# A four-layer cross-attention kernel: the third layer (layer 2) loads the context's means and variances that layer 0 stores

## What is computed

```python
# layer 0
q_c = _ln(x) @ W_qc + b_qc
kv_c = _ln(context) @ W_kvc + b_kvc          # _ln: (x - mean) * rsqrt(var + 1e-6), no weights
# layer 2
xq = _ada_ln(x_q, t_vec, Wss_q, bss_q)
xkv = _ada_ln(x_kv, t_vec, Wss_kv, bss_kv)   # (x - mean) / sqrt(var + 1e-5), then (1 + scale) * . + bias
kv = (xkv @ Wkv + bkv).reshape(B, Lkv, 2, nh, dh)
# layer 3 attends to the context as it is, with no norm of it
```

## Time and profile before

| | |
|---|---|
| median of 3 runs | 5429.4 us (5426.66 to 5432.44) |
| the profiled execution | 5426.89 us, its span 5425.1 us |
| modulation and phase `pa` (layer 0) | up to about 1819 us of the span |
| expert layer (layer 1) | 1823 to 2403 us |
| phase `pb` (layers 2 and 3) | 2407 us to the end |
| busy share of the span | PE 86%, DVE 76%, ACT 66%, POOL 31% |
| DMA | 17% of the 16 engines' span, 50 GB/s |

### The profile page before, as it was taken

How to read it: one execution, slowest core, us unless ns; L and a number is a source line. 1 busy time by engine, 2 the same in 40 slices (tenths; PEclk the granted TensorE clock), 3 DMA queues, 4 the chain that set the end, 5 groups by cost and what they waited for, 6 DMA issues and landing times.

```text
span 5425.1 us, 123295 instructions
## 1 busy us (share of the span) xinstructions
PE 4676.3 (86%) x47956; PEld 2196.8 (40%) x47956; DVE 4123.3 (76%) x8997; ACT 3587.5 (66%) x4899; POOL 1673.2 (31%) x2339
## 2 busy tenths in 40 slices
PE   4689889889998588867989999999999998989987
PEld 2234433433433377752333333333333343333333
DVE  4588888888878244445888888888888887887884
ACT  1377777777777344423777777777777777777776
POOL 3444343343341100024232423233222223232321
PEclk9799999999999899986999999999999999999998
DMA  2211211211210111102112111121211111211110
GB/s 52 68 52 54 68 44 54 67 44 52 61 39 25 45 33 33 33 25 64 52 51 66 55 58 55 53 66 54 67 56 53 51 48 50 62 43 53 42 46 7
DMA packets 362976, 271.12 MB, mean 50 GB/s; under 512 B 47911, under 2 KB 325002, under 8 KB 362396
## 3 DMA queue, kind: packets, MB, share of 16 engines
q1 hardware_dynamic: 362396, 263.23, 17.0%
HBM read 86.96 MB, written 12.78 MB: 18 GB/s over the span
## 4 chain that ended last, share of the span: by engine, by line
PE 36%; ACT 7%; DVE 6%; issue 5%; POOL 1%; SPq 0%; DMA 0%; ACTq 0%; POOLq 0%; DVEq 0%
PE pb_obank L1021 13%; PE pb_dbank L1034 8%; ACT pb_probs L772 6%; DVE pb_c_maxs L693 5%; PE pb_aunit L997 5%; PE pb_aunit L1068 2%; PE pb_aunit L1075 2%; PE pb_dbank L1082 1%; PE pb_aunit L1060 1%; PE pb_aunit L1108 1%; PE pb_aunit L1102 1%; PE pb_aunit L1005 1%; ACT pb_c_kf L815 1%; PE pb_aunit L1051 0%; PE pb_aunit L1092 0%
## 5 line engine op out<-in xcount | busy, mean ns | idle before, releaser
L693 DVE TENSOR_REDUCE pb_c_maxs<-pb_dbank 128x1 f32<-128x512 f32 (+1 forms) x3584 | 2044.5, 627 | 411.6 <-PE pb_dbank L1034 397.1
L772 ACT ACTIVATE pb_probs<-pb_aunit 128x1024 f32<-128x1024 f32 (+1 forms) x1792 | 1744.5, 1024 | 380.4 <-PE pb_aunit L997 344.8
L693 DVE TENSOR_REDUCE pa_c_maxs<-pa_dbank 128x1 f32<-128x512 f32 (+1 forms) x1792 | 1025.8, 627 | 180.2 <-PE pa_dbank L1034 170.5
L772 ACT ACTIVATE pa_probs<-pa_aunit 128x1024 f32<-128x1024 f32 (+1 forms) x960 | 934.8, 1026 | 198.1 <-PE pa_aunit L997 174.8
L1021 PE MATMUL pb_obank<-pb_probs,pb_c_vaug 128*9 128x256 f32 x13312 | 953.2, 384 | 6.3 <-ACT pb_probs L772 5.5
L1034 PE MATMUL pb_dbank<-pb_c_kst,pb_c_qst 62*128 62x512 bf16 (+1 forms) x4096 | 780.5, 344 | 77.1 <-DVE pb_c_maxs L693 67.7
L997 PE MATMUL pb_aunit<-pb_c_qst,pb_c_kst 64*128 64x256 bf16 x6144 | 570.1, 273 | 61.1 <-ACT pb_probs L772 43.1
L1034 PEld LDWEIGHTS pb_dbank<-pb_c_kst,pb_c_qst 62*128 62x128 bf16 x4096 | 233.6, 93 | 632.8 <-DVE pb_c_maxs L693 433.2
L1021 PE MATMUL pa_obank<-pa_probs,pa_c_vaug 128*9 128x256 f32 x6656 | 481.2, 385 | 6.2 <-ACT pa_probs L772 5.8
L1034 PE MATMUL pa_dbank<-pa_c_kst,pa_c_qst 62*128 62x512 bf16 (+1 forms) x2048 | 396.8, 345 | 53.8 <-DVE pa_c_maxs L693 42.6
L1021 PEld LDWEIGHTS pb_obank<-pb_probs,pb_c_vaug 128*9 128x9 f32 x13312 | 245.1, 89 | 375.3 <-issue 214.4
(11 more groups left out here) (475 smaller groups left out, 6680.3 us busy)
## 6 DMA issues: line engine op xcount, KB each, us to landing
pb_c_kst<-pb_c_ksp SPq DMA_DIRECT2D x384, 200.1 KB
pa_c_kst<-pa_c_ksp SPq DMA_DIRECT2D x192, 200.1 KB
pb_c_cin<-in_ctx SPq DMA_DIRECT2D x32, 768.0 KB
pa_c_cin<-in_ctx SPq DMA_DIRECT2D x16, 768.0 KB
moe_cin<-in_ctx SPq DMA_DIRECT2D x16, 768.0 KB
pb_c_qst<-pb_c_qsp SPq DMA_DIRECT2D x384, 32.0 KB
pa_z_qst<-pa_z_qsp SPq DMA_DIRECT2D x192, 32.0 KB
pa_z_kst<-pa_z_ksp SPq DMA_DIRECT2D x192, 32.0 KB
```

The lines of the kernel that those rows point to most:

```text
L693: dve.tensor_reduce(dst, dbank[N % RING_D][:, 0:cnt * width].rearrange("p (s c) -> p s c", s=cnt), AX.X, ALU.max).then_inc(d_free, 1)
L772: act.activation(probs[u % RING_P][0:rows].rearrange("p a i q -> p (a i q)"), src[0:rows, :], ACT.Exp, scale=HD ** -0.5).then_inc(a_free, 1)
```

## The change

Layer 0's spec gets `stats_out` and layer 2's gets `stats_in`, both a new scratch tensor of 16 x 128 x 26 in device memory (13 tiles, mean and variance of each row). A new token "sc" at 0.300, two items ahead, makes SP wait for the aggregates and store `cagg` (phase `pa` only); DVE waits for the store of the item before ahead of overwriting `cagg`. In layer 2 the "cs" tokens leave the list, the "ca" token stays but has no part on DVE, and SP loads `cagg` behind the two context loads of "ldc". POOL waits for that load and for the context's, instead of for DVE. The sixteen loads of 128 rows of 104 bytes come to 13 KB each, and so do the sixteen stores. The costs of the planner's model are not changed.

```diff
@@ -98,7 +98,7 @@
 
 
     def __init__(self, name, keys, x_src, x_dst, wq, wk, wv, wo, bq, bk, bv, bo, eps, ctx=None, ctx_ln=None,
-                 q_cols=None, k_cols=None, gate=None, mlp=None, after=None):
+                 q_cols=None, k_cols=None, gate=None, mlp=None, after=None, stats_in=None, stats_out=None):
         self.name, self.keys, self.x_src, self.x_dst = name, keys, x_src, x_dst
         self.wq, self.wk, self.wv, self.wo = wq, wk, wv, wo
         self.bq, self.bk, self.bv, self.bo = bq, bk, bv, bo
@@ -110,6 +110,8 @@
         self.gate = gate
         self.mlp = mlp
         self.after = after
+        self.stats_in = stats_in
+        self.stats_out = stats_out
 
 
 class Weights:
@@ -287,6 +289,7 @@
             for i in range(4):
                 at(0.100 + 0.04 * i, 2, "cs", i)
             at(0.260, 2, "ca")
+            at(0.300, 2, "sc")
             at(0.360, 2, "ctx", 0)
             at(0.420, 2, "ctx", 1)
             at(0.470, 2, "k", 0)
@@ -332,7 +335,9 @@
             i = b + off + s.lead
             if 0 <= i < len(s.items):
                 spec = s.items[i][0]
-                if tok[0] in ("cs", "ca") and not spec.ctx_ln:
+                if tok[0] in ("cs", "ca", "sc") and not spec.ctx_ln:
+                    continue
+                if tok[0] == "cs" and spec.stats_in is not None or tok[0] == "sc" and spec.stats_out is None:
                     continue
                 if tok[0] == "lda" and not (spec.q_cols or spec.k_cols):
                     continue
@@ -528,6 +533,7 @@
             s.x_in, s.a_cols, s.c_in = sem(f"{m}_x_in"), sem(f"{m}_a_cols"), sem(f"{m}_c_in")
             s.ln_st, s.ln_p, s.x_ln = sem(f"{m}_ln_stats"), sem(f"{m}_ln_small"), sem(f"{m}_x_ln")
             s.c_st, s.c_p, s.c_ln = sem(f"{m}_ctx_stats"), sem(f"{m}_ctx_small"), sem(f"{m}_c_ln")
+            s.stats_kept, s.stats_in = sem(f"{m}_stats_kept"), sem(f"{m}_stats_in")
             s.q_r, s.q_mid, s.q_sp = sem(f"{m}_q_rest"), sem(f"{m}_q_mid"), sem(f"{m}_q_split")
             s.k_hi, s.k_r, s.k_mid, s.k_sp = sem(f"{m}_k_high"), sem(f"{m}_k_rest"), sem(f"{m}_k_mid"), sem(f"{m}_k_split")
             s.q_st, s.k_st = sem(f"{m}_q_stacked"), sem(f"{m}_k_stacked")
@@ -594,6 +600,14 @@
                     src, kt = spec.ctx[n], s.kt
                     sp.dma_start(s.cin[:, 0:kt - 1, :], src[0:(kt - 1) * P, :].rearrange("(t p) d -> p t d", p=P)).then_inc(s.c_in, 16)
                     sp.dma_start(s.cin[0:s.last, kt - 1, :], src[(kt - 1) * P:s.keys, :]).then_inc(s.c_in, 16)
+                    if spec.stats_in is not None:
+                        j = s.norm_to[i]
+                        if j:
+                            sp.wait_ge(s.c_p, 3 * j - 1)
+                        sp.dma_start(s.cagg[:], spec.stats_in[n].rearrange("p (t e) -> p t e", e=2)).then_inc(s.stats_in, 16)
+                elif k == "sc":
+                    sp.wait_ge(s.c_st, 2 * s.kt * (s.norm_to[i] + 1))
+                    sp.dma_start(spec.stats_out[n].rearrange("p (t e) -> p t e", e=2), s.cagg[:]).then_inc(s.stats_kept, 16)
                 elif k == "kq":
                     sp.wait_ge(s.filled, s.fills)
                     if i >= 2:
@@ -633,6 +647,7 @@
                         sp.dma_start(dst, s.x1[:]).then_inc(s.x_out, 16)
             for s in streams:
                 sp.wait_ge(s.x_out, 16 * len(s.items))
+                wait(sp, s.stats_kept, 16 * sum(1 for spec, _ in s.items if spec.stats_out is not None))
 
         @block.vector
         def _(dve):
@@ -651,7 +666,7 @@
 
             dve.memset(obank[:], 0.0).then_inc(ones_set, 1)
             for s in streams:
-                if s.norm_to[-1]:
+                if s.norm_to[-1] and s.items[0][0].stats_in is None:
                     dve.memset(s.cagg[:], 0.0)
                 if s.key not in fill_late:
                     fill(s)
@@ -719,10 +734,12 @@
                         if t * 4 // s.kt == tok[1]:
                             rows = s.last if t == s.kt - 1 else P
                             dve.bn_stats(s.cstats[0:rows, t, :], s.cin[0:rows, t, :]).then_inc(s.c_st, 1)
-                elif k == "ca":
+                elif k == "ca" and spec.stats_in is None:
                     j = s.norm_to[i]
                     dve.wait_ge(s.c_st, 2 * s.kt * j + s.kt)
                     wait(dve, s.c_ln, j * s.kt)
+                    if spec.stats_out is not None:
+                        wait(dve, s.stats_kept, 16 * j)
                     for t in range(s.kt):
                         rows = s.last if t == s.kt - 1 else P
                         dve.bn_aggr(s.cagg[0:rows, t, :], s.cstats[0:rows, t, :]).then_inc(s.c_st, 1)
@@ -887,7 +904,11 @@
                         pool.tensor_scalar(s.xn[:, t, :], s.xin[:, t, :], s.rs_m[:, t:t + 1], s.rs_y[:, t:t + 1], ALU.add, ALU.mult).then_inc(s.x_ln, 1)
                 elif k == "ca":
                     j = s.norm_to[i]
-                    pool.wait_ge(s.c_st, 2 * s.kt * (j + 1))
+                    if spec.stats_in is None:
+                        pool.wait_ge(s.c_st, 2 * s.kt * (j + 1))
+                    else:
+                        pool.wait_ge(s.stats_in, 16 * (j + 1))
+                        pool.wait_ge(s.c_in, 32 * (i + 1))
                     pool.tensor_scalar(s.cs_v[:], s.cagg[:, :, 1], spec.ctx_ln, None, ALU.add).then_inc(s.c_p, 1)
                     pool.tensor_scalar(s.cs_m[:], s.cagg[:, :, 0], -1.0, None, ALU.mult).then_inc(s.c_p, 1)
                     pool.wait_ge(s.c_p, 3 * j + 2)
@@ -1780,25 +1801,26 @@
                          part(b, 0), part(b, 1), part(b, 2), a[prefix + bo], 1e-6,
                          q_cols=(first_col, first_col + 1), gate=gate, after=after)
 
-    def cross(prefix, name, x_src, x_dst, q, q_b, kv, kv_b, wo, bo, eps, ctx_ln, q_cols, k_cols, mlp, after=None):
+    def cross(prefix, name, x_src, x_dst, q, q_b, kv, kv_b, wo, bo, eps, ctx_ln, q_cols, k_cols, mlp, after=None, stats_in=None, stats_out=None):
         w, b = a[prefix + kv], a[prefix + kv_b]
         return Attention(name, S, x_src, x_dst, a[prefix + q], part(w, 0), part(w, 1), a[prefix + wo],
                          a[prefix + q_b], part(b, 0), part(b, 1), a[prefix + bo], eps, ctx=a["ctx_1024"],
-                         ctx_ln=ctx_ln, q_cols=q_cols, k_cols=k_cols, mlp=mlp, after=after)
+                         ctx_ln=ctx_ln, q_cols=q_cols, k_cols=k_cols, mlp=mlp, after=after, stats_in=stats_in, stats_out=stats_out)
 
     def batches(spec):
         return [(spec, n) for n in range(B)]
 
+    stats = scratch("ctx_stats", (B, P, 26))
     p0, p2, p3 = "L0_xcond_", "L2_xcond_", "L3_xcond_"
     l0_self = own(p0, "l0_self", a["x"], xs[0], "W_qkv", "b_qkv", "W_proj", "b_proj", L0_COLS, 0)
     l0_cross = cross(p0, "l0_cross", xs[0], xs[1], "W_qc", "b_qc", "W_kvc", "b_kvc", "W_cproj", "b_cproj", 1e-6, 1e-6, None, None,
                      dict(w1=a[p0 + "W_mlp1"], b1=a[p0 + "b_mlp1"], w2=a[p0 + "W_mlp2"], b2=a[p0 + "b_mlp2"],
-                          cols=(L0_COLS + 2, L0_COLS + 3), gate=1, eps=1e-6), after=("z", 0))
+                          cols=(L0_COLS + 2, L0_COLS + 3), gate=1, eps=1e-6), after=("z", 0), stats_out=stats)
     attention_phase(nc, "pa", [Stream("c", S, batches(l0_cross), 0), Stream("z", NQ, batches(l0_self), 3)], cols, rows, ident, True, {"c": ("ln", "z", 1)})
     expert_layer(nc, {**w1, "wq": a["L1_xcond_Wq"], "wk": a["L1_xcond_Wk"], "wv": a["L1_xcond_Wv"],
                       "gamma": a["L1_xcond_ln_gamma"], "beta": a["L1_xcond_ln_beta"]}, xs[1], xs[2], a["ctx_1024"], cols, rows, ident, B)
     l2_cross = cross(p2, "l2_cross", xs[2], xs[3], "Wq", "bq", "Wkv", "bkv", "Wp", "bp", 1e-5, 1e-5,
-                     (L2_COLS, L2_COLS + 1), (L2_COLS + 2, L2_COLS + 3), None)
+                     (L2_COLS, L2_COLS + 1), (L2_COLS + 2, L2_COLS + 3), None, stats_in=stats)
     l3_self = own(p3, "l3_self", xs[3], xs[4], "qkv_w", "qkv_b", "sa_proj_w", "sa_proj_b", L3_COLS, 2, after=("c", 0))
     l3_cross = cross(p3, "l3_cross", xs[4], out, "q_w", "q_b", "kv_w", "kv_b", "ca_proj_w", "ca_proj_b", 1e-6, None, None, None,
                      dict(w1=a[p3 + "fc1_w"], b1=a[p3 + "fc1_b"], w2=a[p3 + "fc2_w"], b2=a[p3 + "fc2_b"],
```

## The result

The changed kernel took **5414.8 us** (8 runs, 5413.0 to 5422.5), the kernel before, on the same chip, 5431.6 (8 runs, 5426.7 to 5434.7): ratio **0.9973**, 95% interval 0.9963 to 0.9984, a gain of 9 to 20 us. Timed once more, beside other runs of the kernel before, it gave 0.9978 (0.9969 to 0.9988), a gain of 7 to 17 us. The forecast was 5422, a gain of 7, with 5408 to 5435 as its range: the range held, the size was too small, and both ratios lie in the "faster by over 0.2%" to which 0.26 was given, though the second interval reaches out of it.

A forecast was written before the change was run, and what follows sets the result against it. It took DVE to be a partner of PE through three PSUM banks, not plainly the bound. 14 bodies x 0.5 us = 7 us, all else 0, gave 5422 us against the 5429.4 median; range 5408 to 5435.

The forecast's parts named there:

- What bounds the kernel: Second attention phase: DVE is PE's partner through three PSUM banks, not plainly the bound; its maxima hold 8.1% of the chain.
- Rival 1: Second attention phase: DVE is the bound and every microsecond counts, 14 x 3.79 = 53 us gained, 5376; chance 0.04.
- The rehearsal: Last layer-2 bodies, preparing layer-3 items without context norm: 0.76 us shorter; 0.40 to 0.76 credited to statistics and order.
- The leftover charge: Planner still books 2.2 us to DVE for "ca", delaying maxima; taken in the middle, leaning low: 0.5 us a body.
- Rival 2: Order beats the rehearsal's: front stretch not crowded, next still gains 1.33 us; 19 us gained, 5411; chance 0.22.
- Rival 3: Order crowds the front stretch, next gives nothing back: 0.58 us a body, 8 us slower, 5437; chance 0.14.
- the four or so early bodies do as the others: Bodies before self-attention joins were assumed to gain like later ones, PE being busy 91% in both.
- Nothing is gained directly later: POOL starts the norm earlier, but PE's transposes waited for it only twice, 13.6 us, at the start: no direct gain later.
- Body 0: First body of the second attention phase, counted like the other 13 at 0.5 us.
- SP, loads and stores: Added loads cost 0 with 27 us of slack, added first-phase stores 0 with 16 us.
- The casts' price: DVE's c_mbf takes 302 ns beside POOL's norm, 174 without; gain already counted in the rehearsal's 0.76 us.

The follow-up runs named there:

- order only: Kernel before, planner charging nothing for layer 2's "cs": PE's order as in the changed kernel, DVE still making the statistics; 5432.3 us, ratio 0.9998.
- busy kept: Changed kernel, but DVE still issues 13 bn_stats and 13 bn_aggr an item on a constant tile into a spare one; 5428.9 us, ratio 0.9989.
- work only: Changed kernel with "cs" kept in the planner's list and skipped by DVE: old PE order without the work; 5423.5 us, ratio 0.9984.
- Charge 0: Changed kernel without the 2.2 us the planner still books to DVE for "ca" in layer 2; 5423.1 us, ratio 0.9982, steady body 94.51 us.
- plain copies: Charge 0 with layer 2's scale and bias left out of ACT's context copies; 5416.6 us, ratio 0.9976, steady body 94.18 us.
- the charges of 1.1 and 3.3: Changed kernel with the planner's 2.2 us for "ca" on DVE set to 1.1 or 3.3; 5419.1 us (0.9981) and 5429.6 us (0.9996).

## Why the prediction was half right

The path from before over "order only" and "busy kept" to the changed kernel changes one thing at a time (us, from the table):

| | order | POOL's early start | DVE's time | all | forecast |
|---|---|---|---|---|---|
| body 0, second quarter | -1.11 | -0.25 | -1.83 | -3.19 | -0.5 |
| bodies 1-4 | +4.41 | -3.17 | -3.30 | -2.06 | -2.0 |
| bodies 5-13 | -3.90 | -0.16 | -1.60 | -5.66 | -4.5 |
| sum | -0.60 | -3.58 | -6.73 | -10.9 | -7.0 |

Each is one trace against another, so that an entry can be off by what single bodies showed, 0.2 to 1.3 us. These shares hold for this path. Over "work only" DVE and POOL come first and give 6.6 us in the old order, and the new order then gives 4.3.

**What bounds the kernel: right.** DVE is a partner, not the bound. Rival 1 wanted 3.8 us an item and 53 in all. In steady bodies DVE lost 3.3 us of work and the period nothing ("work only"). The rule of the Trainium skill (Perfetto Trace Analysis, Identifying the Most-Contended Engine) named DVE; the trace of this kernel does not bear it out, though in the early bodies, where DVE is busy 69.5 of 79.8 us, its time is felt in part.

**The rehearsal: right, and better than I used it.** Its 0.76 us were split into 0.36 for ACT's copies and 0.40 for statistics and order. "Charge 0" has the order and not the short copies: 94.51, which is 0.43 less than before; "plain copies" gives the other 0.33. The doubt whether PE felt the longer copies is settled: nearly all of it.

**The leftover charge: leaned the wrong way.** "It undoes the rehearsal's gain" was one end, no loss in front the other, and I leaned to the first. It gives 0.17 us, by luck of where the maxima fall, as the charges of 1.1 and 3.3 show. With 0.43 it makes the 0.60 of a steady body, where I had taken 0.5. Rival 2 has the same cause, but not its size: it wanted 28.94 + 27.81, and it was 29.36 + 28.12.

**Rival 3 did happen, in the early bodies.** The new order alone costs 0.81, 0.71, 1.92 and 0.97 us in bodies 1 to 4. POOL's start and DVE's time hide it. That the four or so early bodies do as the others came out right in the sum, -2.1 against -2.0, by luck, and wrong in every part: there the order loses and the removed work gains, the reverse of the steady bodies. I had argued from PE's busy share, 91% in both the earlier trace rows. The share doesn't tell how the engines hand over to each other.

**POOL: the step that read too few rows.** "Nothing is gained directly later" rested on the row of PE's matmuls, two waits of 13.6 us in the start, and these did stay. But an in-order PE also stops where its weight load waits, in a row of its own: 4.8 us in 20 waits in the kernel before, 7.4 in 29 in "order only", 4.2 in 18 in the changed one, from 2400 to 2900 us. The waits are short, 0.3 us at most, as the transposes follow POOL tile by tile; together POOL's start took 3.1 us of them away ("busy kept"), and bodies 1 to 4 got 3.2 shorter.

**Body 0: the mis-sized term.** It was counted at 0.5 us like the rest. Its second quarter gave 3.19, most of what the sum lacks. Windows of 1 us of the kernel before show why:

```profile
2554.00:2555.00 1.00, 0.39 (x1) 0.09 (x1) 1.00 (x2) 1.00 (x2) 0.00 (x0) 1.00 0.00 0
2555.00:2556.00 1.00, 0.20 (x1) 0.09 (x1) 1.00 (x15) 0.68 (x2) 0.00 (x0) 1.00 0.00 0
2556.00:2557.00 1.00, 0.36 (x9) 0.36 (x11) 1.00 (x3) 0.00 (x0) 0.73 (x3) 1.00 0.02 8
2557.00:2558.00 1.00, 1.00 (x12) 0.31 (x12) 0.92 (x4) 0.87 (x1) 1.00 (x1) 0.78 0.00 0
2558.00:2559.00 1.00, 1.00 (x12) 0.34 (x15) 0.96 (x2) 1.00 (x2) 1.00 (x1) 0.50 0.00 0
2559.00:2560.00 1.00, 1.00 (x10) 0.13 (x4) 0.00 (x0) 0.07 (x1) 0.89 (x3) 0.50 0.00 0
2560.00:2561.00 1.00, 1.00 (x10) 0.45 (x6) 0.62 (x2) 0.19 (x1) 1.00 (x3) 0.52 0.07 16
```

For three microseconds DVE is fully busy and PE stands at 0.39, 0.20 and 0.36: 13 `bn_aggr` (0.96 us, from 2555.05) lie ahead of the maxima that PE's banks wait for, and the timeline puts this down as a PE wait of 1.25 us. Then the granted clock falls to 0.50, the 1.2 GHz level, for some three microseconds of full work. In the changed kernel PE is at 0.47 and 0.48 for two microseconds at the same place, and there is no fall:

```profile
2551.00:2552.00 1.00, 0.47 (x7) 0.23 (x7) 1.00 (x4) 1.00 (x2) 0.92 (x2) 1.00 0.00 0
2552.00:2553.00 1.00, 0.48 (x10) 0.21 (x6) 0.15 (x1) 1.00 (x3) 1.00 (x1) 1.00 0.00 0
2553.00:2554.00 1.00, 1.00 (x20) 0.34 (x16) 0.68 (x2) 1.00 (x2) 0.89 (x2) 1.00 0.00 0
2554.00:2555.00 1.00, 1.00 (x18) 0.33 (x10) 0.98 (x3) 0.88 (x2) 1.00 (x3) 1.00 0.00 0
```

The quarter's clock is 0.93 in the traces of all four kernels whose DVE has the 26 extra instructions, and 1.00 in the nine others. The order doesn't decide it. The fall is the whole of what DVE's time was worth there: "busy kept" has the fall in body 0 and not in body 1, with the same matmuls.

```profile
2560.74:2584.56 23.82, 22.16 (x213) 8.45 (x213) 17.73 (x45) 16.99 (x21) 9.68 (x16) 0.93 0.19 48
```

That is 1.82 us more than the 22.00 of body 1, shown above, and the changed kernel's 21.99 is 1.83 less. That the fall goes when DVE's work goes is shown. That the thin stretch of PE causes it is a guess, and thinness alone does not settle it: two microseconds of body 1 of the changed kernel are as thin, with no fall behind them.

```profile
2629.29:2630.29 1.00, 0.41 (x12) 0.27 (x6) 0.94 (x3) 0.82 (x1) 0.75 (x3) 1.00 0.07 16
2630.29:2631.29 1.00, 0.39 (x4) 0.12 (x4) 0.00 (x0) 1.00 (x2) 1.00 (x1) 1.00 0.00 0
```

**SP, loads and stores: right.** Costs of 0 and slack of 15 us and more, as read. First phase, expert layer and layer 3 show no change clear of their spread: the expert layer starts at 1823.7 (1822.8 before; 1822.8 to 1829.2 over all kernels) and takes 578.6 us against 580.0, and bodies 14 to 31 take 1581.7 us against 1581.2.

**Not the change: 2.2 us of the start.** The bodies give 10.9 us of the 13.8 between the spans. Another 2.2 are in the first quarter of body 0, 149.3 us before and 147.0 after. They follow the granted clock, which differs there between runs of one kernel. Twenty microseconds from 65 us ahead of the quarter's end, of the kernel before, the changed one, and the changed one again:

```profile
2490.29:2510.29 20.00, 17.56 (x42) 4.33 (x40) 15.85 (x29) 1.85 (x2) 9.96 (x8) 0.59 0.14 41
2487.51:2507.51 20.00, 16.28 (x46) 4.69 (x45) 17.19 (x32) 2.69 (x3) 9.96 (x8) 0.76 0.17 43
2492.34:2512.34 20.00, 17.61 (x42) 4.32 (x40) 15.72 (x29) 1.86 (x2) 9.97 (x8) 0.59 0.16 42
```

The clock is 0.59 there in the four traces whose first quarter took 148.9 to 150.9 us, two with the statistics in DVE and two without, and 0.76 in the nine that took 146.8 to 147.8. So the profiled pair makes the gain look 2.2 us larger than the change is. Why the clock differs is open.

## What to carry to other kernels

Where engines work in fixed orders written by a planner, taking work off one of them changes two things, the work and the order, and the two can be priced apart: keep the token and skip the work, or keep the work and uncharge the token. Read an in-order engine's waits in both of its rows, matmuls and weight loads, and count the early bodies by themselves, since a busy share that is alike says nothing of what the hand-overs are. Look too for places where a short stall of PE stands just ahead of a fall of its clock: there it may cost more than its own length. And compare the granted clock of the stretches before a difference between two traces is called the change's.

## What the runs showed that I had not expected

- A few microseconds of thin PE work, at 0.39, 0.20 and 0.36 busy, were followed by about three at half clock. Body 1 of the kernel before has the same `bn_aggr` ahead of the maxima and the same PE wait of 1.25 us, and its quarter kept a clock of 1.00; why is open.
- The casts' price moved instead of going away. A `c_mbf` fell from a mean of 299 ns to 174 (two in a body), but a `z_mbf` takes 320, where it took 190, and a `z_mhl` 274, where it took 214. One of the two is slow, and what POOL does beside it is not its norm of the context, as I had read the earlier trace rows, but its work on z's q (`pb_z_qf`), which stands behind the norm in its order and so moves with it (DVE's line, then POOL's):

```profile
3264.61 0.47 DVE L718 CAST pb_z_mbf<-pb_z_negm 128x16 bf16<-128x16 f32 x1
3264.38 0.67 POOL L923 TENSOR_TENSOR pb_z_qf<-pb_z_qf,pb_z_qsp 128x256 f32<-128x256 f32 x1
```

The cast ends 0.03 us after POOL's operation does. In the kernel before the slow `c_mbf`, 0.42 us at 3280.45, lies beside the same operation, and a `z_mbf` that does lie beside the norm takes 0.20 us. The Trainium skill (SBUF — State Buffer, Who interferes with whom) says that a DVE cast in a two-port mode, or a DVE instruction with two SBUF inputs, contends with POOL for a shared pair of ports, and that `tensor_reduce` on this chip never does; the trace agrees on the casts and on `z_mhl`. It is why DVE is busy 79.75 us in a body and not the rehearsal's 79.28.
- Three maxima placed one token later, with the same work on every engine, cost 0.69 us a body, more than all that the change gives in one.
